# Layer 0's key sums from VectorE to ScalarE, TensorE's filler matmuls ahead of their waits, and the wait for the last stores from GpSimd to SyncE

## The reference

```python
# attention of layer 0 (16 heads of 8): q, k, v from LN(x) and ctx
q = split(LN(x) @ Wq.T + bq);  k = split(ctx @ Wk.T + bk);  v = split(ctx @ Wv.T + bv)
p = softmax((q @ k.T * tau + delta) / sqrt(8))
x = x + merge(p @ v) @ Wo.T + bo
# layer 0: relu(x @ wi + lora of the top-1 expert) @ wo;  layer 1: the same attention,
# then 8 experts, each token through the expert of its highest logit, gelu, times that probability
```

## Time and profile before

| what | value |
|---|---|
| time, median of 3 runs | 187.86 us (187.83 to 189.19) |
| time of the profiled execution | 189.11 us |
| its span, first to last instruction | 187.3 us |
| mean granted TensorE clock | 0.967 |
| busy: PE, DVE, ACT, POOL | 165.9 (89%), 122.0 (65%), 97.4 (52%), 72.3 us (39%) |
| DMA | 15.48 MB, mean 83 GB/s |

### The profile page before, as it was taken

The page is one execution under the profiler, slowest core; times in us unless marked ns, Lnnn a source line. Parts: engine busy times, 40 slices in busy tenths (PEclk is TensorE's granted clock), DMA queues, the critical chain, the costliest instruction groups (busy, mean ns, idle before and its releaser), DMA issues.

```text
span 187.3 us, 3431 instructions
## 1 busy us (share of the span) xinstructions
PE 165.9 (89%) x902; PEld 115.9 (62%) x907; DVE 122.0 (65%) x359; ACT 97.4 (52%) x230; POOL 72.3 (39%) x95
## 2 busy tenths in 40 slices
PE   6577999999999977699999988899679999999950
PEld 2433566567655843455955554554568999999940
DVE  2877995689384398938395998652587572964420
ACT  5329184875636135016238834575346766866520
POOL 8899250000404036000010000044366877886861
PEclk9969999999999999669999999999999999999997
DMA  6500003500000000001799930002910248100100
GB/s 181 181 2 4 6 4 72 192 0 0 2 3 0 0 2 4 4 3 11 229 365 455 432 160 0 0 30 85 275 41 7 84 116 258 31 9 5 36 15 0
DMA packets 14483, 15.48 MB, mean 83 GB/s; under 512 B 6842, under 2 KB 11205, under 8 KB 14400
## 3 DMA queue, kind: packets, MB, share of 16 engines
q1 hardware_dynamic: 12944, 13.29, 21.8%
q0 software_dynamic: 1088, 1.60, 2.6%
q10 hardware_dynamic: 432, 0.37, 0.8%
HBM read 13.50 MB, written 5.44 MB: 101 GB/s over the span
## 4 chain that ended last, share of the span: by engine, by line
PE 61%; DVE 14%; issue 10%; POOL 5%; ACT 3%; DMA 2%; POOLq 1%; DVEq 0%; ACTq 0%
PE acc L1022 14%; PE scores L1112 7%; PE acc L1124 7%; PE scores L1007 5%; PE shared L1069 4%; PE shared L1055 4%; PE shared L982 4%; PE shared L964 3%; PE shared L916 3%; POOL out L563 3%; DVE QG L767 2%; DVE XN L729 2%; DVE MR L777 2%; DMA X<-in_x 2%; PE shared L1029 2%
## 5 line engine op out<-in xcount | busy, mean ns | idle before, releaser
L1022 PE MATMUL acc<-P,VP 123*128 123x512 f32 (+1 forms) x80 | 39.8, 595 | 0.4 <-ACT P L641 0.4
L687 ACT ACTIVATE HT<-scores,B 128x128 f32<-128x128 f32 x88 | 25.2, 374 | 10.7 <-PE scores L1112 9.5
L546 POOL TENSOR_TENSOR X<-X,ROWS 128x512 f32<-128x512 f32 x6 | 7.6, 1271 | 59.2 <-DVE XN L729 59.1
L641 ACT ACTIVATE P<-scores 123x512 f32<-123x512 f32 (+1 forms) x40 | 22.9, 596 | 13.8 <-PE scores L1007 13.3
L777 DVE TENSOR_REDUCE MR<-shared 128x4 f32<-128x308 f32 x64 | 27.0, 470 | 3.6 <-PE shared L982 2.9
L563 POOL DMA_INDIRECT out<-XS,token x22 | 22.5, 1022 | 7.3 <-issue 6.0
L1124 PE MATMUL acc<-W,HT 128*128 x176 | 23.1, 278 | 1.3 <-ACT HT L687 1.3
L1112 PE MATMUL scores<-XST,HT 128*128 128x128 f32 x176 | 23.3, 277 | 0.0
L982 PE MATMUL shared<-KG,QG 98*128 98x308 f32 x64 | 22.4, 420 | 0.1
L1124 PEld LDWEIGHTS acc<-W,HT 128*128 128x128 f32 x176 | 21.1, 192 | 1.9 <-issue 1.9
L1007 PE MATMUL scores<-QG,KG 102*123 102x512 f32 (+1 forms) x48 | 21.4, 503 | 0.1
(11 more groups left out here) (123 smaller groups left out, 250.6 us busy)
## 6 DMA issues: line engine op xcount, KB each, us to landing
W<-in_w SPq DMA_DIRECT2D x16, 256.0 KB, 6.6
slots<-in_empty SPq DMA_DIRECT2D x1, 2860.0 KB, 14.0
XS<-slots SPq DMA_DIRECT2D x2, 650.0 KB, 5.6
XS<-slots SPq DMA_DIRECT2D x2, 390.0 KB, 4.3
W<-in_ffn0w SPq DMA_DIRECT2D x1, 534.0 KB, 5.0
XS<-slots SPq DMA_DIRECT2D x2, 260.0 KB, 3.5
X<-in_x SPq DMA_DIRECT2D x2, 256.0 KB, 4.3
B<-in_b SPq DMA_DIRECT2D x1, 512.0 KB, 5.5
```

The source lines that it names most:

```text
L641: act.activation(P[0:w, n % NP], scores[n % 2][0:w, :], ACT.Exp).then_inc(probs_ready, 1)
L687: ins = act.activation(HG1[:, t % NHB, c], hidden[t % 2][:, c], ACT.Gelu_apprx_tanh, bias=B1[:, bass.ds(expert[t] * NF + k, 1)])
L1022: pe.matmul(acc[half][:, :], VP[0:w, l, b, j, half], P[0:w, n % NP, :], start=(j == 0), stop=(j == NT - 1)).then_inc(probs_used, 1)
```

## The change

Three edits. First, the step `kp/0` leaves VectorE's table and enters ScalarE's, ahead of `ks/0`: the four sums of L738 go, and ScalarE's four activations of L609 are made for layer 0 too. Second, in TensorE's steps `q` and `max` the call of `hold` stands ahead of the waits for the step's inputs, so the fillers of that step no longer wait for them; the fillers ahead of the first `max` are 4 where they were 5. Third, the wait for `stored` goes from the end of GpSimd's stream to the end of SyncE's. GpSimd's table is written in another form with the same steps in the same order.

```diff
     "act": """
-        ln/0/0 ks/0 xt/0/0 ln/0/1 q/0/0/0:2 mt/0/0/0 xt/0/1 sc/0/0/0:2 q/0/1/0 sc/0/0/2:4 mt/0/0/1 sc/0/0/4:8
+        ln/0/0 kp/0 ks/0 xt/0/0 ln/0/1 q/0/0/0:2 mt/0/0/0 xt/0/1 sc/0/0/0:2 q/0/1/0 sc/0/0/2:4 mt/0/0/1 sc/0/0/4:8
...
     "dve": """
-        ln/0/0 xn/0/0 kp/0 ln/0/1 vp/0 ks/0 km/0/0 q/0/0/0:2 max/0/0/0:8 xn/0/1 mt/0/0/0 max/0/0/8:14 q/0/1/0
+        ln/0/0 xn/0/0 ln/0/1 vp/0 ks/0 km/0/0 q/0/0/0:2 max/0/0/0:8 xn/0/1 mt/0/0/0 max/0/0/8:14 q/0/1/0
...
-FILL = {('q', 0, 0, 0): 6, ('max', 0, 0, 0): 5, ('max', 0, 0, 3): 5, ('max', 0, 0, 4): 1, ('max', 0, 0, 5): 1, ('max',
+FILL = {('q', 0, 0, 0): 6, ('max', 0, 0, 0): 4, ('max', 0, 0, 3): 5, ('max', 0, 0, 4): 1, ('max', 0, 0, 5): 1, ('max',
...
                     sp.dma_start(XS[:, t0:t1], sv[:, t0:t1]).then_inc(slots_in[b][i], 16)
+            sp.wait_ge(stored, 16 * NS)
...
-            pool.wait_ge(stored, 16 * NS)
...
                 elif kind == "kp":
                     l = s[1]
+                    act.wait_ge(in_wk if l == 0 else in_att[l], 16)
                     if l == 1:
-                        act.wait_ge(in_att[l], 16)
                         act.wait_ge(k_split, B)
-                        for g in range(G):
-                            key = (*s, g // 2)
-                            read(act, key)
-                            act.activation(Kf[:, g], k_of(key, g), ACT.Identity,
-                                           bias=ATT[l][0:QR, A_BK + g:A_BK + g + 1]).then_inc(k_biased, 1)
+                    for g in range(G):
+                        key = (*s, g // 2)
+                        read(act, key)
+                        act.activation(Kf[:, g], k_of(key, g), ACT.Identity,
+                                       bias=ATT[l][0:QR, A_BK + g:A_BK + g + 1]).then_inc(k_biased, 1)
...
-                elif kind == "kp":
-                    l = s[1]
-                    if l == 0:
-                        dve.wait_ge(in_wk, 16)
-                        for g in range(G):
-                            key = (*s, g // 2)
-                            read(dve, key)
-                            dve.tensor_scalar(Kf[:, g], k_of(key, g), ATT[l][0:QR, A_BK + g:A_BK + g + 1], None,
-                                              ALU.add).then_inc(k_biased, 1)
...
                 elif kind == "q":
                     _, l, b, pair = s
+                    hold(s)
                     pe.wait_ge(in_att[l], 16)
                     pe.wait_ge(xnt_ready, nth["xt", 2 * l, b] + 1)
-                    hold(s)
...
                 elif kind == "max":
                     _, l, b, i = s
                     n = nth[s]
                     g, qt = divmod(i, NQ)
+                    hold(s)
                     if qt == 0:
                         pe.wait_ge(ql_ready, 2 * nth["q", l, b, g // 2] + g % 2 + 1)
...
-                    hold(s)
                     off = PAD * (g % 2)
```

More of the change, by code:

```diff
@@ L107 @@
     "pool": """
-        one/0 pre/0/0 km/0/1 pre/0/1 one/1 pre/1/0 km/1/0 pre/2/0 km/1/1 pre/1/1 pre/2/1 row/0/0 row/0/1 row/0/2 row/0/3 ln/3/1 pb/0:8 so/0 pb/8:10 so/1 pb/10 row/1/0 row/1/1 row/1/2 row/1/3 so/2 so/3 so/4 so/5 pb/11 so/6 pb/12 so/7 pb/13 so/8 pb/14 so/9 pb/15 so/10
-        pb/16 so/11 so/12 pb/17 so/13 pb/18 so/14 pb/19 so/15 pb/20 so/16 so/17 so/18 pb/21
-        so/19 so/20 so/21
+        one/0 pre/0/0 km/0/1 pre/0/1 one/1 pre/1/0 km/1/0 pre/2/0 km/1/1 pre/1/1 pre/2/1 row/0/0:4 ln/3/1 pb/0:8
+        so/0 pb/8:10 so/1 pb/10 row/1/0:4 so/2:6 pb/11 so/6 pb/12 so/7 pb/13 so/8 pb/14 so/9 pb/15 so/10 pb/16
+        so/11:13 pb/17 so/13 pb/18 so/14 pb/19 so/15 pb/20 so/16:19 pb/21 so/19:22
     """,
 }
-FILL = {('q', 0, 0, 0): 6, ('max', 0, 0, 0): 5, ('max', 0, 0, 3): 5, ('max', 0, 0, 4): 1, ('max', 0, 0, 5): 1, ('max',
+FILL = {('q', 0, 0, 0): 6, ('max', 0, 0, 0): 4, ('max', 0, 0, 3): 5, ('max', 0, 0, 4): 1, ('max', 0, 0, 5): 1, ('max',
         0, 0, 6): 1, ('mt', 0, 0, 0): 5, ('wo', 0, 1): 7, ('q', 1, 0, 0): 3, ('xt', 1, 1): 5, ('max', 1, 0, 2): 1,
```

## The result

The changed kernel takes 186.42 us (median of 6 runs, 184.96 to 188.57), the kernel before 188.61 in 6 runs beside it (187.83 to 189.86; the three shown ahead were the first of them). The ratio is 0.9897, 95% interval 0.9848 to 0.9947: faster by about 1%, clear of no change but under 2%, 1.9 us by the ratio and 2.2 by the medians. (A ratio leaves out runs that lie over 1.5% above the fastest of their kernel, and medians here are over all runs, so the two can differ.) The forecast was 185.3, range 184.2 to 187.5, a gain of 2.6 us. Later runs of the kernel before had medians of 187.75 (23 runs) and 188.25 (11).

What follows compares the result with a forecast made beforehand. The prediction saw the kernel bound by a chain of waits at the start, with a late GpSimd DRAIN at the end. Early gain -1.96, clock +0.5, end -1.1 sum to -2.6 us: from 187.86 to 185.3, range 184.2 to 187.5.

Steps and rivals of the forecast that it cites:

- the two ends: VectorE's `Ks` split: held by GpSimd's delta operation (gain 1.96 us, taken), or held only by the semaphore at `KG` (2.72).
- The row of 1235 ns: Normalized row at 71.08, median 340 ns, ending just behind GpSimd's `KG` pair; cited as evidence that GpSimd blocks VectorE.
- The rival with a gain of 2.72: VectorE's split runs beside GpSimd's operation, early gain 2.72 us, time 184.5; chance 0.07.
- Idle time behind the fillers: TensorE idles 1.0 us ahead of the first `max` and another 1.6 us ahead of the fourth.
- I take 0.5, nearer to the end without a fall: Clock cost of TensorE's idle time around the first maxima, taken as 0.5 us between 0 and 1.3.
- rows of 131.50: Stretch 131.50 to 133.50: TensorE busy 0.46 of 2.00 us, clock stayed at 1.00; the case for no fall.
- the row of 6.83: Stretch 6.83 to 10.45: TensorE busy 0.63 of 3.62 us, clock fell at 11.2; the case for a fall.
- The end: After the last scatter: GpSimd's DRAIN starts at 183.3 while SyncE takes the wait for stores; gain 1.1 us.
- The rival in which it waits for the stores: GpSimd's closing DRAIN waits for the stores, so the last edit only renames the waiter; 186.4 us, chance 0.15.
- Layer 1 at nothing: Moving the three fillers of layer 1's first query gains nothing, since VectorE is in normalized rows until 73.
- The slower rival: Clock falls in the new idle time at 12.7 to 16.05 and stays low; price 3.4, 188.2 us, chance 0.10.
- The rival on the early low stretch of before: Low clock 11.2 to 14.6 is only the profiled execution's excess over the median; early gain 0.7, 186.6 us, chance 0.13.

Runs made afterwards that it cites:

- e6: Changed kernel with GpSimd's delta chain moved ahead of the memset of `VP[:, 0]`; one execution, 183.88 us.
- e2: Changed kernel with layer 0's key sums back on VectorE, fillers still ahead of the waits; one execution, 188.15 us.
- e3: Changed kernel with fillers of `q` and `max` back behind the waits, five ahead of the first `max`, other two edits kept; one execution, 183.38 us.
- e1: Changed kernel with the wait for `stored` back at the end of GpSimd's stream; one execution, 190.44 us.
- e8: Changed kernel with only layer 1's query fillers back behind the wait; 187.15 us (12 runs), ratio 0.9933.
- e5: The same kernel as e3, timed on another chip; 184.64 us (6 runs), ratio 0.9831.

## Why the prediction was right in its direction, and where its sizes were off

- **Where `KG` and the low parts land: right.** `XNT` from 8.53 (forecast 8.45), split's end 11.4, `KG`'s end 12.94, low parts 12.97, maxima 16.07. The choice between the two ends (split held by GpSimd, or free) was right, and e6 shows the cause: with GpSimd's operation moved, the split ends at 10.2 and the low parts start at 11.79. The row of 1235 ns that it leaned on is of an operation with one tensor input, where the split has two; it bears the reading out only by likeness, and e6 is the test. The rival with a gain of 2.72 fell: it would have needed the split to end at 10.2.
- **Credit for it: not separated.** The text read as if the moved sums and the moved fillers each contributed. e2 and e3 show that with either of them the low parts start where they do with both.
- **Idle time behind the fillers: right in place** (forecast 1.0 and 1.6 us, measured 1.47 and 1.15), and "it would be wrong if the clock is low anywhere between 14 and 21" is what happened.
- **"I take 0.5, nearer to the end without a fall": the step that failed.** The profile has 1.58, at the fall's end of the range and above its 1.3, as the fourth maximum and those behind it slow down too. I had chosen by rows of 131.50, where the clock stayed up beside a busy time of 0.46 in 2.00 us; the row of 6.83 (0.63 of 3.62, and a fall right behind) was the nearer one, in length and place.
- **The end: right, a little small.** 1.1 by subtraction of the wait, 1.32 measured. The forecast counted up to the branch at 184.4 and took off 0.1 for the start; but the DRAIN began at 184.5, 1.3 us behind the last issue, and now it ends 2.5 behind that issue, as if it had begun at its end. Of the signs, "starts 0.1 us behind its last scatter and takes 2.5 us" failed to the letter, and "if the DRAIN grows by the wait it lost" came true as written: 3726 ns are 1.2 more than 2529. But the 1.2 lie at its front, beside the issue, and not at its end. The rival in which it waits for the stores fell: it would end 3.8 us behind the issue as before, and ends 2.5 behind it; e1 puts the wait back and has 3.8.
- **Layer 1 at nothing: right for the query, not for the stretch.** The low stretch there was 3.4 us instead of 6.8 in the profiled execution, which gave 0.8. e1, which is the changed kernel up to the last scatter, was low there for 6.8 us, so the length varies between executions, and I don't book the 0.8 to the change.
- **The slower rival: its mechanism exists, its sum doesn't carry.** The fall of 6.8 us came in e1 and e8 and cost 2.3 to 2.5 us at the transposed maxima, against e3, rather than 3.4. Less the 1.96 and the 1.3 it is still no loss.
- **The rival on the early low stretch of before: its mechanism is there, how often is open.** The fastest run of the kernel before (185.37, clock 0.992) lies 2.3 us above the fastest of e5 (183.07, 0.997) and 2.0 above e3 (183.38, 0.996), not 3.3. In the profiles the mean clock follows from the low time: before, 12.3 us of 187.3 are at half the clock (from 11.20, 76.06 and 185.28 on), which gives 0.967. By that, 0.992 leaves about 3 us of low clock in the whole run, less than one stretch of 3.4, and so no early one. An early gain of 0.55 to 0.7 and the 1.3 of the end give 1.9 to 2.0. No trace of such an execution was taken, and in how many runs of the kernel before the early stretch is absent stays open.
- **The number.** Against 186.42 the forecast is 1.1 us low. About 0.75 of it is the base: the three runs had a median of 187.86, the six 188.61. The rest is that the medians lie 2.2 us apart and not 2.6; the two profiled executions lie 2.8 apart, since the profile of before was 0.5 above its median. The terms themselves add up to -2.8 in the profiles, close to the forecast's -2.6, but in part by luck: the clock term was 1.1 too small, and 0.8 in layer 1, 0.3 among the experts and 0.2 at the end, none of them in the sum, made up for it.

## What to carry to other kernels

Filler matmuls belong into the idle time, neither behind the wait, where they lengthen the path (0.3 us at the fourth `max`, 1.19 at the gate), nor in too small a number ahead of it, where they are gone when the idle time comes; so count the wait in fillers and read the granted clock behind it, in more than one execution. When two edits each remove the same wait, look up what ends last after one of them before booking the second. And an engine whose closing DRAIN is long shouldn't be the one that waits for the last stores.

## What was not expected of the hardware

- GpSimd's DRAIN takes 2529 ns when all stores have landed, and SyncE's 7 ns (130 ns before and 122 in e1, where SyncE's stream ends near 155 us). With the wait on SyncE, GpSimd's is recorded from ahead of the last scatter's issue with 3726 ns, and ends 2.5 us behind that issue.
- A VectorE operation of 526 ns can take 1658 beside one GpSimd operation of 1.5 us, and 529 beside GpSimd's memset of 2.23 us; a normalized row of 340 ns can take 1358 beside GpSimd's `KG` pair (e6).
- The low stretches last 3.4, 6.8 or 10.2 us in these traces (16.04 to 19.45, 14.66 to 21.48, 72.86 to 83.1), and the empty waits ahead of the one in the changed kernel were no longer than 1.47 us each. The same kernel's mean clock varies from one execution to the next, 0.955 to 0.992 in 23 runs of the kernel before, and its time with it (190.08 and 185.37 us).
